# Loads of x into layer 2's sums issued one per step over ten steps, with the bias added as each lands

## The reference

```python
def _rgcn_conv(x, src, dst, etype, W, root, b):
    seg = dst * num_rel + etype
    sums = segment_sum(x[src], seg, num_segments=num_nodes * num_rel)
    mean = sums / jnp.maximum(cnt, 1.0)[:, None]          # per node and relation
    out = jnp.einsum('nri,rio->no', mean, W)
    return out + x @ root + b

h = relu(_rgcn_conv(x, src, dst, edge_type, W1, root1, b1))
out = _rgcn_conv(h, src, dst, edge_type, W2, root2, b2)
return _layernorm(x + out, axis=-1)
```

## Time and profile before

| | before |
|---|---|
| median of 3 runs | 1613.88 us (1611.52 to 1614.21) |
| the profiled execution's time | 1614.64 us |
| its span | 1612.9 us |
| TensorE busy | 1515.5 us (94%) |
| VectorE busy | 1127.2 us (70%) |
| ScalarE busy | 671.1 us (42%) |
| GpSimd busy | 690.6 us (43%) |
| mean granted TensorE clock | 0.978 |

### The profile page before, as it was taken

The page is one execution under the profiler, slowest core; times in us unless marked ns, Lnnn a source line. Parts: engine busy times, 40 slices in busy tenths (PEclk is TensorE's granted clock), DMA queues, the critical chain, the costliest instruction groups (busy, mean ns, idle before and its releaser), DMA issues.

```text
span 1612.9 us, 24359 instructions
## 1 busy us (share of the span) xinstructions
PE 1515.5 (94%) x9003; PEld 1485.7 (92%) x9003; DVE 1127.2 (70%) x1725; ACT 671.1 (42%) x935; POOL 690.6 (43%) x515
## 2 busy tenths in 40 slices
PE   5999998999999999999899599999999999899996
PEld 5999998998989999899889599999999999899996
DVE  6879999928988567889890012656565656588696
ACT  3222243314555445575451110544444444357541
POOL 1111111316778455766530330536353636477460
PEclk9999999999999999999999799999999999999998
DMA  5353221234666556766543431556465646567552
GB/s 166 115 186 122 83 69 34 70 128 145 175 222 200 169 181 217 226 212 179 165 151 129 157 104 39 181 164 204 157 205 164 204 163 215 164 195 242 159 156 96
DMA packets 109222, 254.42 MB, mean 158 GB/s; under 512 B 18375, under 2 KB 81526, under 8 KB 109062
## 3 DMA queue, kind: packets, MB, share of 16 engines
q0 software_dynamic: 38400, 136.49, 28.5%
q1 hardware_dynamic: 70726, 116.65, 21.3%
HBM read 243.77 MB, written 65.45 MB: 192 GB/s over the span
## 4 chain that ended last, share of the span: by engine, by line
PE 61%; DVE 19%; DMA 12%; issue 3%; ACT 2%; POOL 1%; SPq 1%; ACTq 0%; POOLq 0%; DVEq 0%
PE prod L672 49%; PE agg L700 9%; DVE g_low L927 5%; DMA y<-y_stage 5%; DMA raw<-y,bucket_index 4%; DVE g_high L927 3%; DMA x_rows<-in_x 3%; DVE acc L934 2%; DVE keyed L1115 2%; DVE slot_hot L1119 2%; DVE one_hot L921 2%; PE agg L809 1%; POOL raw L433 1%; ACT g_high L527 1%; DVE w_low L891 1%
## 5 line engine op out<-in xcount | busy, mean ns | idle before, releaser
L433 POOL DMA_INDIRECT raw<-y,bucket_index x480 | 615.1, 1282 | 530.1 <-DVE g_low L927 307.9
L672 PE MATMUL prod<-w_high,h_high 128*128 128x384 f32 x2160 | 735.8, 341 | 27.3 <-ACT y_stage L560 18.1
L672 PE MATMUL prod<-w_low,h_high 128*128 128x384 f32 x2160 | 729.4, 338 | 0.0
L672 PE MATMUL prod<-w_high,h_low 128*128 128x384 f32 x2160 | 727.9, 337 | 0.0
L927 DVE TENSOR_TENSOR g_low<-raw,g_high 128x768 fp32r<-128x768 f32 x320 | 293.6, 954 | 239.3 <-ACT g_high L527 204.9
L527 ACT ACTIVATE g_high<-raw 128x768 fp32r<-128x768 f32 x480 | 376.8, 839 | 192.7 <-PE agg L700 118.6
L672 PEld LDWEIGHTS prod<-w_high,h_high 128*128 128x128 f32 x2160 | 411.0, 190 | 31.5 <-ACT y_stage L560 19.6
L672 PEld LDWEIGHTS prod<-w_low,h_high 128*128 128x128 f32 x2160 | 410.9, 190 | 0.0
L672 PEld LDWEIGHTS prod<-w_high,h_low 128*128 128x128 f32 x2160 | 410.4, 190 | 0.0
L560 ACT ACTIVATE y_stage<-prod 128x384 f32<-128x384 f32 x280 | 137.3, 491 | 630.8 <-PE prod L672 565.3
L700 PE MATMUL agg<-g_high,one_hot 128*128 128x384 f32 x960 | 251.7, 343 | 25.6 <-DVE g_low L927 17.6
(11 more groups left out here) (107 smaller groups left out, 621.1 us busy)
## 6 DMA issues: line engine op xcount, KB each, us to landing
y<-y_stage SPq DMA_DIRECT2D x280, 187.5 KB
w_raw<-in_w_all SPq DMA_DIRECT2D x36, 1152.0 KB
raw<-y,bucket_index POOLq DMA_INDIRECT x480
x_rows<-in_x SPq DMA_DIRECT2D x10, 375.0 KB
y<-in_x SPq DMA_DIRECT2D x1, 3750.0 KB, 14.7
y<-acc SPq DMA_DIRECT2D x10, 375.0 KB
acc<-in_x SPq DMA_DIRECT2D x10, 375.0 KB
out<-acc SPq DMA_DIRECT2D x10, 375.0 KB
```

The lines of the kernel that those rows point to most:

```text
L433: pool.indirect_dma_start(raw[:, slot_of, :], None, y[0:written * N, :], bass.IndirectOffsetOnAxis(ap=bucket_index[:, r * RT + i:r * RT + ...
L672: mm = pe.matmul(prod[:, bank, 0:HALF], left[:, k, t * P:(t + 1) * P], right[:, h, k, :], start=(k == 0 and left is h_high and right is w_ ...
```

## The change

SP issued the ten loads of x in pairs, behind the stores of steps 3 to 7, on one semaphore for all. Now it issues one behind each of the stores of steps 3 to 12, each tile with its own semaphore. POOL waited for all ten loads before its first addition; now it waits for one tile at a time.

```diff
-        residual_loaded = sem("residual_loaded")
+        residual_loaded = [sem(f"residual_loaded{t}") for t in range(T)]
...
-                if 3 <= s < 3 + T // 2:
-                    for t in (2 * (s - 3), 2 * (s - 3) + 1):
-                        sp.dma_start(acc[0:ROWS[t], t, :], x[t * NT:t * NT + ROWS[t], :])\
-                            .then_inc(residual_loaded, 16)
+                if 3 <= s < 3 + T:
+                    t = s - 3
+                    sp.dma_start(acc[0:ROWS[t], t, :], x[t * NT:t * NT + ROWS[t], :])\
+                        .then_inc(residual_loaded[t], 16)
                 if s == 8:
                     load_unit(ROOT2, 0)
                 if s == 14:
                     load_unit(ROOT2, 1)
...
-            pool.wait_ge(residual_loaded, 16 * T)
             pool.wait_ge(bias_loaded, 32)
             for t in range(T):
+                pool.wait_ge(residual_loaded[t], 16)
                 pool.tensor_tensor(acc[:, t, :], acc[:, t, :], bias[:, 1, :], ALU.add).then_inc(x_biased, 1)
```

## The result

| | before | changed |
|---|---|---|
| median (13 runs each) | 1613.88 us (1608.16 to 1621.09) | 1607.49 us (1597.04 to 1613.87) |
| profiled execution | 1614.64 us, span 1612.9 | 1613.87 us, span 1612.1 |

The ratio is 0.9948, with a 95% interval of 0.9926 to 0.997: 8.4 us faster, between 5 and 12 (the two medians differ by 6.4 us). A second set of runs of the same kernel gave 0.9929 (0.9904 to 0.9954), 11.5 us. The forecast was 11.4 us and a time of 1602.5 us. The first set's median of 1607.49 us lies inside the stated range of 1599 to 1609, but 2 us above the 1605.5 us that the forecast gave itself at most; the second set's median was 1604.62 us.

A forecast was written before the change was run, and what follows sets the result against it. Transfers in one in-order DMA stream hold TensorE through ACT: first weights, then store 15. Root product 3 ends at 935.7 instead of 947.16 us, an 11.4 us gain carried to the end: 1602.5 us from 1613.88, range 1599 to 1609.

The forecast's parts named there:

- The first weights land 12.5 us earlier: First root weights on SP's stream: six loads ahead instead of ten, landing at 904.9 us against 917.4.
- The unknown price of single loads: Single loads between stores on SP's stream: taken as no extra cost; at most 0.3 us each, 3 us by store 15.
- TensorE restarts 2.6 us behind the weights, at a low clock: TensorE after the first weights land: restart at 907.5 us, with 2.3 us kept for the low clock.
- Store 15 decides when root product 3 starts: Store 15 lands at 932.0 us, so root product 3 starts at 932.6, 0.7 us later than TensorE could.
- Root product 1 is held for 0.3 us by stage 17: Root product 1 needs stage 17's bank, thus store 13, landing at 925.1 us and staged at 925.6; costs 0.3 us.
- one stream at a fixed rate: DMA transfers of loads and stores run in issue order: 1.53 us a store, 3.12 us a load.
- The bias costs nothing: POOL's bias additions: last load lands at 923.5 us, last addition done at 925.6, cover 28 us, no cost.
- The rest moves as a block: Everything behind the changed stretch, through 1390.87 us and the later waits, moves 11.4 us ahead.
- part given back in the queue: Rival, 12 in 100: single loads between stores cost 0.4 us each, store 15 at 936.0, gain 7.4, 1606.5 us.
- No change: Rival, 8 in 100: first weights land no earlier, TensorE restarts at 919.94 us, time 1613.9 us.
- slower: Rival, 5 in 100: a store waits for the single load ahead to complete, ten times; 1622.5 us at 2.0 us each.
- an estimate of 2.65 us a load and 1.32 us a store: Alternative queue rate from the Trainium skill: stores drained long before TensorE wants them, gain of four loads, 10.6 us.

The follow-up runs named there:

- loads from step 7: Changed kernel with the loads of x behind the stores of steps 7 to 16 instead of 3 to 12; 1599.5 us, ratio 0.99.
- second weights late: Changed kernel with the second half of the root weights loaded behind store 19 instead of store 14; ratio 0.9931 to the kernel before.
- waits only: Kernel before, loads of x still in pairs, with only the change's semaphore per tile and ten separate POOL waits; ratio 1.0002.
- order only: Kernel before with one load of x per step over ten steps, keeping one semaphore and one POOL wait; ratio 0.9941.
- loads late, one wait: As loads late, but POOL waits for all ten loads before its first addition; 1610.4 us, ratio 0.9971 to the kernel before.
- loads late: Changed kernel with the loads of x behind the stores of steps 10 to 19 instead of 3 to 12; 1589.5 us, ratio 0.9841, second set 0.9843.

## Why the prediction was right, step by step

- **The first weights land 12.5 us earlier** (forecast 904.9 against 917.4): 34.5 instead of 47.3 us behind stage 4, 12.8 us. Right. The store period between stages 8 and 11 was 4.5 where 4.65 was said, and a load between two stores cost 2.9 to 3.0 us, not 3.12. The unknown price of single loads was nothing, the value taken.
- **TensorE restarts 2.6 us behind the weights, at a low clock**: right; root product 0 ended 54.6 us behind stage 4, where 925.4 - 870.06 = 55.3 was forecast.
- **Store 15 decides when root product 3 starts**: this step failed, though its number was right. Store 15 landed 61.9 us behind stage 4 (forecast 61.9), but in neither profile did root product 3 wait for it: stage 19 was done 2.3 and 0.7 us before root product 2 ended. The one run in which it holds TensorE is *loads from step 7*.
- **Root product 1 is held for 0.3 us by stage 17**: this term was mis-sized, and it is the second bound in place of store 15. Stage 17 came 6.05 us behind stage 16 instead of 4.65, and 0.9 us later than the whole sum has it. TensorE stood for 2.0 us and lost the clock in the first profile, and for 1.0 us at full clock in the second; root product 1 took 7.0 and 4.4 us from end to end. That is why the stretch gave 9.3 us once and 11.3 us once, against 11.4. What failed is the premise of one stream at a fixed rate, in which nothing that is issued later can delay a transfer; *second weights late* shows that the second weights did.
- **How near the sum came is luck in part**: between the ends of root products 0 and 3 it has 1.0 us of waiting, 0.3 at product 1 and 0.7 at product 3. The profiles have 3.9 and 1.3 us, all at product 1. Root product 3 ended 67.8 and 65.9 us behind stage 4, where 65.6 was forecast.
- **Small slips in the sums**, none of which moves the forecast: store 13 comes to 925.0, not 925.1; a half of weights brings each engine as many bytes as 2.05 stores if a store has a third of 16 engines (1.9 only with five); the high part of the second weights would be ready at about 934.6, not 935.2.
- **The bias costs nothing**: right for the order of the change (*waits only*, *order only*), with a cover that *loads late, one wait* takes away. The additions ran from 881.1 to 929.5, apart, where 878 to 925 was forecast (3.2 us of it is the later stage 4).
- **The rest moves as a block**: right over sets of runs, where the gains in the stretch and in the time agree. In one pair of profiles it can't be seen: the stretch was 6.4 us ahead at 1391 us, the end 0.8 us.
- **The rivals**: "part given back in the queue" was priced by a cost for each single load, which isn't there; what was given back came from the weights. The interval of the first set alone, 5 to 12 us, doesn't rule out this rival's 7.4 us. "No change" and "slower" have nothing for them: counted from stage 4, SP issued the first weights 12.7 us earlier and they landed 12.8 us earlier. By the rate per engine in the Trainium skill (DMA: Bandwidth & Descriptors, Specifications) the prediction had an estimate of 2.65 us a load and 1.32 us a store, with stores drained long before TensorE wants them. The runs decide against that: a load took 2.9 to 3.0 us and a store 1.5, and store 13 did hold root product 1. The 10.6 us of that estimate can't be told from 11.4 by the times.

## What to carry to other kernels

On this queue, whose transfers land nearly in order, what a transfer costs is decided by who waits for what stands behind it, and the second weights cost something to what stood ahead of them too. Moving ten loads that nobody needs for 50 us behind the stores and weights that an engine waits for was worth 25 us here; spreading it finely, as this change does, got under half of that. Work out the landing of the two or three transfers that are waited for, for each order, before choosing one; and wait per tile when a late order needs it.

## What the runs showed of the hardware

The low part of a half of weights on DVE (two inputs in SBUF) takes 2.56 us. In both profiles with the changed order and one wait it met POOL's additions in a row and took 10.5 and 10.6 us. The first, with POOL's additions beside it (timeline of DVE, then of POOL):

```profile
939.18 10.53 DVE L891 TENSOR_TENSOR w_low<-w_raw,w_high 128x2304 fp32r<-128x2304 f32 x1 [0.73 <-ACT w_high L519]
949.63 1.94 DVE L913 TENSOR_TENSOR acc<-prod,acc 128x384 f32<-128x384 f32 x4
```

```profile
934.59 12.71 POOL L501 TENSOR_TENSOR acc<-acc,bias 128x768 f32<-128x768 f32 x7
```

It ended 2.4 us behind the last addition, so DVE got next to nothing done until POOL had ended, over more than four additions of 1.8 us, none of which was slowed. The gather that POOL issued next (L433) took 3.17 us, and 3.15 in the second profile, where those behind it took 1.00. The sums from PSUM (L913), with one input in SBUF, kept their 0.56 us beside the same additions. The Trainium skill (SBUF — State Buffer, "Who interferes with whom") states that a DVE instruction with two inputs in SBUF contends with a GpSimd instruction that reads SBUF, over a shared pair of ports that is an exclusive lock. That agrees with these rows, and here the loser was shut out over several instructions in a row. In *loads late, one wait* the same two met as well and it took only 3.70 us, and before the change 2.98 us. In these two cases the wait went the other way: one of POOL's additions took 4.1 and 4.2 us. In *loads late* and its second set it took 3.22 and 3.50 us. What decides between the outcomes stays open.

In the changed kernel SP had about six transfers outstanding and was then held in issuing, so it issued the first weights at 891.84 us, 16 us ahead of their landing, much the same distance as before (901.36 to 917.36).
